# One Trainium2 core, a four-part transformer block: gate products placed between large products, some transposes issued by SyncE, earlier output weights

## The chip, the cores and the metric
The kernel runs on one core of a Trainium2 chip. The metric is device time in microseconds (us) of one execution, lower is better. A core has TensorE (PE; its weight loads are shown as PEld), VectorE (DVE), ScalarE (ACT), GpSimd (POOL) and SyncE (SP), each with a queue of its own, worked off in order; a queue can also issue DMAs (SPq, ACTq, POOLq).

## What is computed
Two batches of 512 tokens of 1024 features pass four sub-blocks, each added to the residual `x`:

```python
x = x + tanh(g_xattn[0]) * L0_xattn(layernorm(x), ctx)   # product of two fake-quantised matrices
x = x + tanh(g_ffn[0]) * L0_ffn(layernorm(x))            # W_org plus softmax-weighted LoRA experts
x = x + tanh(g_xattn[1]) * L1_xattn(layernorm(x), ctx)   # 32 query heads, 8 key heads, 1024 keys, then @ Wo
x = x + tanh(g_ffn[1]) * L1_ffn(layernorm(x))            # mixture of experts
# L1_ffn(h):
logits = concat([h, ratio]) @ gate_w + gate_b            # 3 experts; ratio = mean |h| of text / of vision rows
top_val, top_idx = top_k(softmax(logits), 2)             # the values are used per token,
expert(e) = act_e(h @ w1[e] + b1[e]) @ w2[e] + b2[e]     # the indices of token 0 for the whole batch
```

## The kernel before, in words
Every fp32 product is made of three bf16 ones (`triple`, L637): upper × upper, upper × lower, lower × upper part. The token rows stand in eight tiles of 128 (`TT` = 8, tiles 0 to 3 are batch 0). `XTh` and `XTl` hold the upper and lower parts of the normalised rows, transposed by DMA. A weight chunk of 128 rows is loaded by SyncE into one of the stages (`load_weights` L350, `load_expert` L477), gets its upper part from one engine and its lower part from GpSimd, and the semaphore `wt_done` counts finished chunks. All engines are programmed by hand, in program order, with semaphores between them.

The stages around the change, in order:

- **Queries.** 16 items (`query_item` L828) of 24 products of 512 columns, with score products of the first attention groups among them. An item goes to one of the four banks 6, 7, 2, 3; ScalarE copies the upper part (L1280), VectorE takes the lower (L1644, counted by `q_lo`), SyncE stores both to DRAM (`queries_out` L419). SyncE loads one chunk of the output weights `o` after every second item (L456); GpSimd splits it (L516, L518).
- **Attention groups.** 16 groups of 32 steps (`group` L933). A step has a score product (L866), whose maximum VectorE takes (L1616), and the transposed scores of another group (L948), exponentiated by ScalarE (L1261) into a ring of four buffers `PB`; every four steps `weigh` (L879) makes eight narrow fp32 products. GpSimd adds pairs of `PB` buffers (L607), four additions per group. The 17th exponential of a group sequence waits for the first addition, since it overwrites its input. Before group 0, TensorE waits for all 16 lower query halves (`q_lo`, L969).
- **Output tiles.** `output_tile(t)` (L915), 48 products each (L911), for tiles 0 to 7. VectorE updates `X` (L1664), takes mean and variance (`statistics`), ScalarE the root (`root` L1081), VectorE the reciprocal and `xn` (L1683). `rows_turned` (L1164) on ScalarE copies the upper part (L1173), issues its transpose (L1175), sums absolute values (L1178) and issues the transpose of the lower part (L1181), which VectorE makes (`lower_part`, L1595) once the lower transpose of the tile before has landed. In this order, the root of tile t+1 comes behind the lower transpose of tile t.
- **Gate.** `gate_logits(b)` (L975): for four tiles and eight feature chunks a `triple` with 3 output columns, 96 products, then one fp32 product with ones over the absolute sums (L986). `gate_logits(0)` stands between output tiles 5 and 6, `gate_logits(1)` behind the first four hidden tiles. VectorE's `choose_experts(b)` (L1709) needs both results and writes `idx`, which SyncE reads as the address of the expert's weights.
- **First layer of expert slot 0.** Four hidden tiles at once, chunk by chunk (k = 0 to 7, L1041), each k waiting for its w1 chunk; then hidden tiles 4 to 7 one by one (`hidden_tile` L1005), each waiting for the activation (ScalarE, L1319) four tiles before. For the first 16 expert chunks ScalarE makes the upper part (`weights_hi` L1291, L1295), GpSimd the lower (L629); chunks 0 to 11 stand in ScalarE's program among the rows of tiles 5 to 7 (L1304) and ahead of the activations. There are four stages, so the load of chunk c waits for `wt_done` of chunk c − 4. Chunks 8 to 15 are w2.
- Then the second layer, and the other three slots.

Of the kernel before, what the change touches and what calls it, by code (L numbers as in the profile page):

```python
# [14 lines left out]
BF16 = mybir.dt.bfloat16  # L15
# [5 lines left out]
P = 128  # L21
# [95 lines left out]
def build(nc, x, ctx_nat, ctx_t, wts, lora_q, lora_keys, scalars, gate_w, w1, b1, w2, b2, out):  # L117
    with ExitStack() as ctx:
        def sb(name, shape, dt):
            return ctx.enter_context(nc.sbuf_tensor(name, shape, dt))  # L120
# [41 lines left out]
        gwh = sb("gwh", [P, KT * EXPERTS], BF16)  # L162
        gwl = sb("gwl", [P, KT * EXPERTS], BF16)
# [470 lines left out]
        def _(pe):  # L634
# [298 lines left out]
            def group(g):  # L933

                for t in range(STEPS):
# [33 lines left out]
            pe.wait_ge(q_lo, B * KT)  # L969
# [5 lines left out]
            def gate_logits(b):  # L975
                rows_in_place(2, range(b * TB, (b + 1) * TB))
                pe.wait_ge(rt_read, b)
                for t in range(b * TB, (b + 1) * TB):
                    for k in range(KT):
                        cols = slice(k * D + t * P, k * D + (t + 1) * P)  # L980
                        e3 = slice(k * EXPERTS, (k + 1) * EXPERTS)
                        mm = triple([bank[6][:, t * EXPERTS:(t + 1) * EXPERTS]], XTh[:, cols], XTl[:, cols],
                                    [gwh[:, e3]], [gwl[:, e3]], k == 0, k == KT - 1)
                mm.then_inc(lg_mm, 1)
                pe.wait_ge(am_done, 4 * (b + 1))
                pe.matmul(bank[7][:, b * 2 * TB:(b + 1) * 2 * TB], onesf[:, :],  # L986
                          AM[:, b, :, :].rearrange("p a t -> p (a t)"), start=True, stop=True).then_inc(as_mm, 1)
# [53 lines left out]
            for k in range(KT):  # L1041
                pe.wait_ge(wt_done, W1_N(0) + k + 1)
                for f in range(4):
                    if k == 0 and f % 2 == 0:
                        pe.wait_ge(x_up, 6 * TT - 2 + f)
                    w = slice(k * D + f * P, k * D + (f + 1) * P)
                    mm = triple([bank[f][:, :]], w1_h[:, w], w1_l[:, w], [XTh[:, k * D:k * D + S]],
                                [XTl[:, k * D:k * D + S]], k == 0, k == KT - 1)
                    if k == KT - 1:
                        mm.then_inc(a_mm, 1)  # L1050
            gate_logits(1)
# [11 lines left out]
        def _(act):  # L1063
# [100 lines left out]
            def rows_turned(m, t, rooted=False, before_lower=lambda: None):  # L1164

                if not rooted:
                    root(TT + m, t % 2)
# [5 lines left out]
                act.activation(nat_h, xn[0][:, :], ACT.Copy).then_inc(nat_hi, 1)  # L1173
                act.wait_ge(nat_hi, m - TT + 1)
                act.dma_start_transpose(out=per_tile(XTh)[:, :, t * P:(t + 1) * P], in_=nat_h).then_inc(hi_t[t], 16)  # L1175
                if m >= 2 * TT:
                    act.wait_ge(abs_done, t + 1)
                    act.activation(junk, xn[0][:, :], ACT.Abs, accum_out=rowabs[:, t:t + 1]).then_inc(abs_done, 1)  # L1178
                before_lower()
                act.wait_ge(nat_lo, m - TT + 1)  # L1180
                act.dma_start_transpose(out=per_tile(XTl)[:, :, t * P:(t + 1) * P], in_=nat_l).then_inc(lo_t[t], 16)  # L1181

# [46 lines left out]
            for t in range(TT):  # L1229
                rows_turned(TT + t, t)  # L1230
# [66 lines left out]

            for t in range(TT - 3):
# [36 lines left out]
        def _(dve):  # L1335
# [103 lines left out]
            def gate_parts():  # L1439
                dve.wait_ge(const_in, 48)  # L1440
                dve.tensor_copy(gwh[:, :], gwf[:, :]).then_inc(qc_step, 1)
                dve.wait_ge(qc_step, 10)
                dve.tensor_tensor(gwl[:, :], gwf[:, :], gwh[:, :], ALU.subtract).then_inc(qc_step, 1)
# [214 lines left out]
            def output_norm(t):  # L1658
# [7 lines left out]
                dve.wait_ge(x_up, 2 * (m + 1))  # L1666
                statistics(m + TT, x_tile(t), t % 2)
# [41 lines left out]
            def choose_experts(b):  # L1709
# [12 lines left out]
                nxt(dve.tensor_tensor(L[:, tiles, :],  # L1722
                                      bank[6][:, b * TB * EXPERTS:(b + 1) * TB * EXPERTS].rearrange("p (t e) -> p t e", e=EXPERTS),
                                      rb[:, b:b + 1, :].to_broadcast([P, TB, EXPERTS]), ALU.add))
# [151 lines left out]
```

## Time and profile before
| | |
|---|---|
| three runs | 1251.49, 1257.41, 1254.35 us; median 1254.35 |
| the profiled execution | 1259.31 us, its span 1257.5 us, mean granted TensorE clock 0.993 |
| busy: TensorE, VectorE, GpSimd, ScalarE | 1222.9, 821.9, 681.7, 476.4 us |

The span runs from the first to the last instruction. Matmul records of 512 columns show about 0.38 us each, but successive ones start 0.216 us apart; distances between starts are what counts. The granted clock is 1.0 at 2.4 GHz and 0.5 at 1.2 GHz.

### The profile page before, as it was taken

What the parts mean: (1) busy time and instruction counts of PE and PEld (TensorE: products, weight loads), DVE (VectorE), ACT (ScalarE), POOL (GpSimd) and SP (SyncE); (2) the same over time, 40 slices, a digit from 0 to 9 for tenths busy, and PEclk for the clock granted to TensorE, in tenths of its full rate; (3) what the DMA queues carried; (4) which work ended last, traced back from release to release, by engine and by line L of the source; (5) the groups of instructions that cost most, each with busy time, mean ns of one, the idle gap of its engine ahead of it and who ended that gap; (6) DMA issues with size and microseconds to landing.
All of it is one profiled execution on the core that took longest, in us unless ns stands there. A gap on an engine that the chain in (4) does not pass through costs nothing.

```text
span 1257.5 us, 16924 instructions
## 1 busy us (share of the span) xinstructions
PE 1222.9 (97%) x6504; PEld 512.1 (41%) x6504; DVE 821.9 (65%) x1417; ACT 476.4 (38%) x826; POOL 681.7 (54%) x300
## 2 busy tenths in 40 slices
PE   8998899999999899999999999999989999999998
PEld 6564444444444322222222222234434444444444
DVE  7997731433456778998999989335538855737622
ACT  4774521000100467777777677743242010010000
POOL 6005898500033478888989889870164553624510
PEclk9999999999999999999999999999989999999999
DMA  9566143311332145453545444443493443523301
GB/s 356 171 245 154 65 134 115 86 34 34 79 129 92 59 96 113 107 117 87 120 106 112 95 103 104 84 84 60 113 213 105 140 126 100 184 85 101 117 15 52
DMA packets 86764, 141.20 MB, mean 112 GB/s; under 512 B 49056, under 2 KB 59296, under 8 KB 82592
## 3 DMA queue, kind: packets, MB, share of 16 engines
q1 hardware_dynamic: 45840, 94.03, 23.7%
q0 software_dynamic: 4608, 33.56, 13.2%
q10 hardware_dynamic: 36240, 12.60, 5.2%
q8 instruction: 48, 0.79, 0.3%
q14 instruction: 28, 0.23, 0.1%
HBM read 85.49 MB, written 10.49 MB: 76 GB/s over the span
## 4 chain that ended last, share of the span: by engine, by line
PE 79%; DVE 12%; DMA 2%; POOL 2%; ACT 2%; issue 1%; ACTq 0%; SPq 0%; POOLq 0%; DVEq 0%
PE bank L641 46%; PE bank L879 9%; DVE mxp L1616 8%; PE bank L866 6%; PE bank L948 5%; PE bank L911 5%; PE bank L666 3%; PE bank L672 3%; DVE xn L1606 2%; DMA stage_c<-w_in 1%; DMA R<-R 1%; POOL R L607 1%; POOL R L629 1%; PE bank L720 1%; POOL X L548 1%
## 5 line engine op out<-in xcount | busy, mean ns | idle before, releaser
L1616 DVE TENSOR_REDUCE mxp<-bank 128x1 f32<-128x512 f32 x512 | 320.6, 680 | 60.6 <-PE bank L866 60.3
L1261 ACT ACTIVATE R<-bank 128x512 f32<-128x512 f32 x512 | 273.9, 602 | 116.7 <-PE bank L948 113.5
L641 PE MATMUL bank<-XTh,R 128*128 128x512 bf16 x896 | 279.3, 381 | 4.7 <-POOL R L629 4.5
L607 POOL TENSOR_TENSOR R<-R 128x2048 f32<-128x2048 f32 x48 | 218.6, 4555 | 35.4 <-ACT R L1261 29.4
L641 PE MATMUL bank<-R 128*128 128x512 bf16 x960 | 209.2, 379 | 0.0
L641 PE MATMUL bank<-XTl,R 128*128 128x512 bf16 x448 | 170.7, 381 | 0.0
L629 POOL TENSOR_TENSOR R<-stage_pair,R 128x1024 bf16<-128x1024 f32 x32 | 75.4, 2371 | 138.6 <-DVE R L1770 84.1
L641 PEld LDWEIGHTS bank<-R 128*128 128x128 bf16 x960 | 93.9, 98 | 113.3
L866 PE MATMUL bank<-R 96*128 96x512 bf16 x352 | 134.6, 382 | 4.6 <-DVE mxp L1616 3.0
L879 PE MATMUL bank<-R,stage_c 128*32 128x512 f32 x1024 | 137.1, 607 | 0.5 <-ACT R L1261 0.5
L948 PE MATMUL bank<-R 98*128 98x512 bf16 x352 | 134.4, 382 | 2.1 <-ACT R L1261 2.1
L641 PEld LDWEIGHTS bank<-XTh,R 128*128 128x128 bf16 x896 | 88.0, 98 | 112.1 <-POOL R L629 5.4
L516 POOL TENSOR_TENSOR R<-stage_pair,zero 128x1024 f32 (+1 forms) x35 | 67.2, 1920 | 77.4 <-DMA stage_pair<-wts_in 74.5
L629 POOL TENSOR_TENSOR R<-stage_c,R 128x1024 bf16<-128x1024 f32 x32 | 73.7, 2315 | 59.8 <-DVE R L1770 50.2
L1319 ACT ACTIVATE R<-bank,b1t 128x512 f32<-128x512 f32 x32 | 21.6, 686 | 198.1 <-PE bank L641 198.1
L866 PEld LDWEIGHTS bank<-R 96*128 96x128 bf16 x352 | 34.2, 97 | 112.2 <-DVE mxp L1616 84.7
L518 POOL TENSOR_TENSOR R<-stage_pair,R 128x1024 f32 (+1 forms) x35 | 75.9, 2167 | 5.3 <-POOL R L516 4.7
L1606 DVE RECIPROCAL xn<-p_total 128x128 f32<-128x128 f32 x64 | 59.2, 937 | 27.6 <-POOL xn L589 27.6
L607 POOL TENSOR_TENSOR stage_pair<-R 128x2048 f32<-128x2048 f32 x16 | 73.7, 4604 | 4.3 <-ACT R L1261 3.2
L911 PE MATMUL bank<-R,XTh 128*128 128x512 bf16 x256 | 69.7, 379 | 0.8 <-issue 0.8
L1815 DVE SCALAR_TENSOR_TENSOR X<-xn,TV,X 128x512 f32<-128x512 f32 x32 | 67.4, 2147 | 0.1
L1084 ACT ACTIVATE lnv<-lnv 128x1 f32<-128x1 f32 x32 | 6.5, 202 | 158.7 <-DVE lnv L1365 138.3
(194 smaller groups left out, 1502.0 us busy)
## 6 DMA issues: line engine op xcount, KB each, us to landing
stage_pair<-wts_in SPq DMA_DIRECT2D x35, 512.0 KB, 3.7
R<-R POOLq DMA_DIRECT2D x16, 1024.0 KB, 6.9
stage_pair<-R POOLq DMA_DIRECT2D x16, 1024.0 KB, 7.0
stage_pair<-w_in SPq DMA_DIRECT2D x32, 512.0 KB, 3.5
stage_c<-w_in SPq DMA_DIRECT2D x32, 512.0 KB, 3.6
R<-q_scr SPq DMA_DIRECT2D x48, 128.0 KB, 2.4
XTh<-ctx_t_in SPq DMA_DIRECT2D x11, 512.0 KB, 7.7
XTh<-ctx_nat_in SPq DMA_DIRECT2D x9, 512.0 KB, 3.9
```

Source lines behind the costliest of these rows:

```text
L518: pool.tensor_tensor(lo, stage_w[stage][:, :], hi, ALU.subtract).then_inc(wt_done, 1)
L607: pool.tensor_tensor(PS[(0, 1, 2, 1)[j]], PB[2 * j % 4], PB[2 * j % 4 + 1], ALU.add).then_inc(p_add, 1)
L629: pool.tensor_tensor(lo[:, cols], stage_e[(n - N_WT) % RING_E][:, :], hi[:, cols], ALU.subtract).then_inc(wt_done, 1)
L641: mm = pe.matmul(o, a, m, start=first and a is ah and bs is bh, stop=last and a is al)
L866: pe.matmul(bank[s_bank(u)][:, :], QS[g % 3][0:96, h * S + qt * P:h * S + (qt + 1) * P], KS[g % 3][0:96, kh * HALF:(kh + 1) * HALF], start ...
L879: mm = pe.matmul(out_bank[h * HD:(h + 1) * HD, :], weights, probs[:, h * S:(h + 1) * S], start=first, stop=last)
L911: mm = pe.matmul(outs[h], a[i][:, cols], b[i][:, k * D + h * HALF:k * D + (h + 1) * HALF], start=k == 0 and i == 0, stop=k == KT - 1 and i ...
L948: pe.matmul(bank[t_bank(g, t)][:, :], KS[g % 3][0:98, kt * P:(kt + 1) * P], QS[g % 3][0:98, h * S:(h + 1) * S], start=True, stop=True).the ...
L1261: act.activation(PB[kt % 4][:, h * S:(h + 1) * S], bank[t_bank(g, t)][:, :], ACT.Exp, scale=float(HD) ** -0.5).then_inc(exp_done, 1)
L1606: dve.reciprocal(rec[:, cols], p_sum[:, cols]).then_inc(rec_done, 1)
L1616: dve.tensor_reduce(mxp[head // REP % 2][:, m, n // 2, n % 2:n % 2 + 1], bank[s_bank(u)][:, :], AX.X, ALU.max).then_inc(s_max, 1)
L1815: dve.scalar_tensor_tensor(out=xh, in0=b2b[:, hc], scalar=TV[:, j * TT + t:j * TT + t + 1], in1=xh, op0=ALU.mult, op1=ALU.add).then_inc(eo ...
```

## The change
1. Gate products: upper and lower gate weights stand side by side in one tile `gwb`, so that per tile and chunk there are two products (`XTh` with 6 columns, `XTl` with 3) instead of three. They are issued one at a time, each behind a large product: for batch 0 behind the 48 of output tile 5 and the first 16 of tile 6, for batch 1 among the hidden tiles' `triple`s and, the last 16, behind them. VectorE adds the two column sets in one more small operation. Chunks 6 and 7 of the first layer are taken tile by tile, with one wait for both.
2. SyncE issues both transposes of tiles 5, 6 and 7, among the loads of w1 chunks 4 to 7 and ahead of those of w2; it waits for the transposes of tile 4 first. ScalarE only makes the upper parts, and has another order of conversions.
3. ScalarE takes the root of tile t+1 ahead of the lower transpose of tile t; VectorE updates `X` for tile 5 ahead of the expert choice.
4. The `o` weights are loaded after each of the first eight query items. Group 0 starts at 14 lower query halves; its first two steps wait for 15 and 16.

```diff
@@ SyncE
-                if c % 2 == 1:
-                    load_weights(WT_AT["o"] + item // 2, 1)
+                if item < KT:
+                    load_weights(WT_AT["o"] + item, 1)
...
+            def turn_upper(t):
+                sp.wait_ge(nat_hi, TT + t + 1)
+                sp.dma_start_transpose(out=per_tile(XTh)[:, :, t * P:(t + 1) * P], in_=nat_h).then_inc(hi_t[t], 16)
+
+            def turn_lower(t):
+                sp.wait_ge(nat_lo, TT + t + 1)
+                sp.dma_start_transpose(out=per_tile(XTl)[:, :, t * P:(t + 1) * P], in_=nat_l).then_inc(lo_t[t], 16)
+
             e = expert(0)
-            load_expert(W1_N(0), w1, e, 0, KT)
+            load_expert(W1_N(0), w1, e, 0, RING_E)
+            sp.wait_ge(hi_t[TT - 4], 32)
+            sp.wait_ge(lo_t[TT - 4], 32)
+            turn_upper(TT - 3)
+            turn_lower(TT - 3)
+            load_expert(W1_N(0), w1, e, RING_E, RING_E + 1)
+            turn_upper(TT - 2)
+            load_expert(W1_N(0), w1, e, RING_E + 1, KT)
+            turn_lower(TT - 2)
+            turn_upper(TT - 1)
+            turn_lower(TT - 1)
@@ TensorE
-            def output_tile(t):
+            def output_tile(t, gate_parts=range(0)):
...
                 for k in range(KT):
-                    mm = output_part(t, k, 0, 6)
-                mm.then_inc(nat_mm, 1)
+                    for n in range(6):
+                        mm = output_part(t, k, n, n + 1)
+                        if k == KT - 1 and n == 5:
+                            mm.then_inc(nat_mm, 1)
+                        if 6 * k + n < len(gate_parts):
+                            gate_part(0, gate_parts[6 * k + n])
...
+                    elif STEPS * g + t < 2:
+                        pe.wait_ge(q_lo, B * KT - 1 + t)
...
-            pe.wait_ge(q_lo, B * KT)
+            pe.wait_ge(q_lo, B * KT - 2)
...
-            def gate_logits(b):
...
+            def gate_part(b, n):
+
+                t, k, low = b * TB + n // (2 * KT), n // 2 % KT, n % 2
+                if n % (2 * KT) == 0:
+                    rows_in_place(2, range(t, t + 1))
+                if n == 0:
+                    pe.wait_ge(rt_read, b)
+                cols = slice(k * D + t * P, k * D + (t + 1) * P)
+                count = EXPERTS if low else 2 * EXPERTS
+                mm = pe.matmul(bank[6][:, 2 * t * EXPERTS:2 * t * EXPERTS + count], (XTl if low else XTh)[:, cols],
+                               gwb[:, 2 * k * EXPERTS:2 * k * EXPERTS + count], start=k == 0 and not low,
+                               stop=k == KT - 1 and low == 1, skip_group_check=True)
+                if n == 2 * KT * TB - 1:
+                    mm.then_inc(lg_mm, 1)
...
-            for t in range(TB, TT - 2):
-                output_tile(t)
-            gate_logits(0)
-            for t in range(TT - 2, TT):
-                output_tile(t)
+            output_tile(TB)
+            output_tile(TB + 1, range(0, 48))
+            output_tile(TB + 2, range(48, 64))
+            output_tile(TB + 3)
...
+            for k in range(KT - 2):
                 pe.wait_ge(wt_done, W1_N(0) + k + 1)
                 for f in range(4):
...
-            gate_logits(1)
+                    first_part(f, k)
+                    if k < 4:
+                        gate_part(1, 8 * k + 2 * f)
+                        gate_part(1, 8 * k + 2 * f + 1)
+            pe.wait_ge(wt_done, W1_N(0) + KT)
+            for f in range(4):
+                for k in range(KT - 2, KT):
+                    first_part(f, k)
+                    gate_part(1, 32 + 4 * f + 2 * (k - KT + 2))
+                    gate_part(1, 33 + 4 * f + 2 * (k - KT + 2))
+            for n in range(48, 64):
+                gate_part(1, n)
@@ ScalarE
             for t in range(TT - 3):
-                if t == 0:
-                    divided_hi(GROUPS - 1)
-                rows_turned(2 * TT + t, t, rooted=t == 0)
+                if t > 0:
+                    root(3 * TT + t, t % 2)
+                    turn_lower(2 * TT + t - 1, t - 1)
+                rows_upper(2 * TT + t, t)
+                turn_upper(2 * TT + t, t)
+                absolute_sum(t)
+            root(4 * TT - 3, 1)
+            turn_lower(3 * TT - 4, TT - 4)
...
-            for t, before, after in ((TT - 3, (0, 2), (2, 2)), (TT - 2, (4, 2), (6, 1)), (TT - 1, (7, 1), (8, 4))):
-                rows_turned(2 * TT + t, t, before_lower=lambda before=before: weights_hi(*before))
-                weights_hi(*after)
+            rows_upper(3 * TT - 3, TT - 3)
+            absolute_sum(TT - 3)
+            root(4 * TT - 2, 0)
+            weights_hi(0, 2)
+            rows_upper(3 * TT - 2, TT - 2)
+            absolute_sum(TT - 2)
+            weights_hi(2, 2)
+            root(4 * TT - 1, 1)
+            weights_hi(4, 2)
+            rows_upper(3 * TT - 1, TT - 1)
+            absolute_sum(TT - 1)
+            weights_hi(6, 6)
@@ VectorE
             for t in range(TB + 1):
+                output_up(t)
                 output_norm(t)
             absolute_sums(0)
+            output_up(TB + 1)
             choose_experts(0)
-            for t in range(TB + 1, TT):
+            output_norm(TB + 1)
+            for t in range(TB + 2, TT):
+                output_up(t)
                 output_norm(t)
```

## Rows read from the trace of the kernel before

**Rows 1.** the page: the span of the profiled execution
```profile
span 1257.5 us, 16924 instructions
```
**Rows 2.** the chain of waits in order of time: start us, us, what
```profile
425.58 3.75 DMA stage_pair<-wts_in
...
914.52 10.35 DMA stage_c<-w_in
...
933.29 2.13 POOL R L629
...
943.42 310.83 PE bank L641 x1440
```
**Rows 3.** TensorE in time, 424 to 443: start, us, what, [idle before <- releaser]
```profile
424.77 0.39 PE L866 MATMUL bank<-R 96*128 96x512 bf16 x1 [1.42 <-DVE R L1644]
...
433.97 1.06 PE L879 MATMUL bank<-R,stage_c 128*32 128x512 f32 x8
...
438.93 0.39 PE L948 MATMUL bank<-R 98*128 98x512 bf16 x1 [2.06 <-ACT R L1261]
439.25 1.80 PE L879 MATMUL bank<-R,stage_c 128*32 128x512 f32 x8
...
442.98 0.38 PE L948 MATMUL bank<-R 98*128 98x512 bf16 x1
```
**Rows 4.** GpSimd in order of time, 429 to 443 us
```profile
429.50 1.89 POOL L516 TENSOR_TENSOR R<-stage_pair,zero 128x1024 f32 x1 [8.05 <-DMA stage_pair<-wts_in]
...
433.65 8.99 POOL L607 TENSOR_TENSOR R<-R 128x2048 f32<-128x2048 f32 x2
```
**Rows 5.** ScalarE in order of time, 429 to 439 us
```profile
429.92 2.06 ACT L1261 ACTIVATE R<-bank 128x512 f32<-128x512 f32 x4 [0.94 <-PE bank L948]
...
438.28 0.60 ACT L1261 ACTIVATE R<-bank 128x512 f32<-128x512 f32 x1 [2.07 <-POOL R L607]
```
**Rows 6.** TensorE in time, the first gate group, 888 to 891 us
```profile
888.86 0.17 PE L641 MATMUL bank<-gwh,XTh 128*128 128x3 bf16 x1
...
891.28 0.37 PE L986 MATMUL bank<-AM,onesf 128*128 128x8 f32 x2
```
**Rows 7.** TensorE in order of time, the stop at the eighth first-layer weight
```profile
935.46 0.61 PE L641 MATMUL bank<-XTh,R 128*128 128x512 bf16 x1 [4.50 <-POOL R L629]
...
940.56 0.21 PE L641 MATMUL bank<-gwh,XTh 128*128 128x3 bf16 x1
```
**Rows 8.** DMA issues of 918 to 919.4 us: us from issue to landing
```profile
XTl<-xn ACTq DMA_TRANSPOSE x1, 13.3
```
**Rows 9.** all engines in order of time, first product behind the second gate group
```profile
943.16 0.18 PEld L641 LDWEIGHTS bank<-XTh,R 128*128 128x128 bf16 x1
943.27 0.38 PE L641 MATMUL bank<-XTh,R 128*128 128x512 bf16 x1
```
**Rows 10.** VectorE in order of time, 895 to 912 us
```profile
895.15 0.16 DVE L1738 CAST idx<-idxf 1x2 int32<-1x2 f32 x1
...
898.30 1.22 DVE L1595 TENSOR_TENSOR xn<-xn 128x1024 bf16<-128x1024 f32 x1
...
911.56 0.81 DVE L1683 TENSOR_SCALAR xn<-X,mv,lnv 128x1024 f32<-128x1024 f32 x1
```
**Rows 11.** SyncE's queue in order of time: first load of an expert's weights
```profile
896.11 0.95 SPq L481 DMA_DIRECT2D stage_pair<-w_in  x2
```
**Rows 12.** DMA issues, 898 to 902 us: KB, us from issue to landing
```profile
stage_c<-w_in SPq DMA_DIRECT2D x1, 512.0 KB, 6.9
XTl<-xn ACTq DMA_TRANSPOSE x1, 6.2
```
**Rows 13.** ScalarE and its queue in order of time, 915 to 941 us
```profile
915.85 1.04 ACT L1295 ACTIVATE R<-stage_pair 128x1024 bf16<-128x1024 f32 x1
...
918.37 1.25 ACTq L1181 DMA_TRANSPOSE XTl<-xn  x1
...
940.25 1.28 ACT L1319 ACT_TABLE_LOAD   x1
```

More of the change, by code:

```diff
@@ L161, in build @@
         gwf = sb("gwf", [P, KT * EXPERTS], F32)
-        gwh = sb("gwh", [P, KT * EXPERTS], BF16)
-        gwl = sb("gwl", [P, KT * EXPERTS], BF16)
+        gwb = sb("gwb", [P, KT * 2 * EXPERTS], BF16)
         b1t = sb("b1t", [P, EXPERTS * KT], F32)
@@ L972, in _ @@
                 group(g)
-            def gate_logits(b):
[L976 to L987, printed above, removed]
+            def gate_part(b, n):
[11 more added lines that the diff above has]
+                    mm.then_inc(lg_mm, 1)
+                    pe.wait_ge(am_done, 4 * (b + 1))
+                    pe.matmul(bank[7][:, b * 2 * TB:(b + 1) * 2 * TB], onesf[:, :],
+                              AM[:, b, :, :].rearrange("p a t -> p (a t)"), start=True, stop=True).then_inc(as_mm, 1)
             weigh(GROUPS - 1, KT - 1)
@@ L1038, in second_layer, with first_part @@
                         mm.then_inc(b_half if halves == (0,) else b_mm, 1)
-            for k in range(KT):
+            def first_part(f, k):
+                if k == 0 and f % 2 == 0:
+                    pe.wait_ge(x_up, 6 * TT - 2 + f)
+                w = slice(k * D + f * P, k * D + (f + 1) * P)
+                mm = triple([bank[f][:, :]], w1_h[:, w], w1_l[:, w], [XTh[:, k * D:k * D + S]],
+                            [XTl[:, k * D:k * D + S]], k == 0, k == KT - 1)
+                if k == KT - 1:
+                    mm.then_inc(a_mm, 1)
+            for k in range(KT - 2):
                 pe.wait_ge(wt_done, W1_N(0) + k + 1)
                 for f in range(4):
[L1044 to L1050, printed above, removed]
-            gate_logits(1)
+                    first_part(f, k)
[10 more added lines that the diff above has]
+                gate_part(1, n)
             for f in range(4, KT):
@@ L1162, in _, with rows_upper @@
             act.wait_ge(const_in, 48)
-            def rows_turned(m, t, rooted=False, before_lower=lambda: None):
-                if not rooted:
-                    root(TT + m, t % 2)
+            def rows_upper(m, t):
                 act.wait_ge(xn_done, TT + m + 1)
@@ L1173, in rows_turned, with turn_upper, turn_lower, absolute_sum @@
                 act.activation(nat_h, xn[0][:, :], ACT.Copy).then_inc(nat_hi, 1)
+            def turn_upper(m, t):
                 act.wait_ge(nat_hi, m - TT + 1)
                 act.dma_start_transpose(out=per_tile(XTh)[:, :, t * P:(t + 1) * P], in_=nat_h).then_inc(hi_t[t], 16)
[L1176 to L1179, printed above, removed]
+            def turn_lower(m, t):
                 act.wait_ge(nat_lo, m - TT + 1)
                 act.dma_start_transpose(out=per_tile(XTl)[:, :, t * P:(t + 1) * P], in_=nat_l).then_inc(lo_t[t], 16)
+            def absolute_sum(t):
+                act.wait_ge(abs_done, t + 1)
+                act.activation(junk, xn[0][:, :], ACT.Abs, accum_out=rowabs[:, t:t + 1]).then_inc(abs_done, 1)
             def scale_rows(t):
@@ L1229, in _ @@
             for t in range(TT):
-                rows_turned(TT + t, t)
+                root(2 * TT + t, t % 2)
+                rows_upper(TT + t, t)
+                turn_upper(TT + t, t)
+                turn_lower(TT + t, t)
             def row_out(g):
@@ L1296, in weights_hi @@
                                    ACT.Copy).then_inc(ew_act, 1)
+            divided_hi(GROUPS - 1)
             for t in range(TT - 3):
[L1299 to L1301 removed]
+                if t > 0:
[6 more added lines that the diff above has]
+            turn_lower(3 * TT - 4, TT - 4)
             act.wait_ge(pv_mm, KT * GROUPS)
             act.wait_ge(p_add, KT // 2 * GROUPS)
[L1304 to L1306 removed]
+            rows_upper(3 * TT - 3, TT - 3)
[10 more added lines that the diff above has]
+            weights_hi(6, 6)
             reg = act.alloc_register("expert_act")
@@ L1440, in gate_parts @@
                 dve.wait_ge(const_in, 48)
-                dve.tensor_copy(gwh[:, :], gwf[:, :]).then_inc(qc_step, 1)
+                full = gwf[:, :].rearrange("p (k e) -> p k e", k=KT)
+                gw_h, gw_l = (gwb[:, :].rearrange("p (k i e) -> p i k e", k=KT, i=2)[:, i, :, :] for i in range(2))
+                dve.tensor_copy(gw_h, full).then_inc(qc_step, 1)
                 dve.wait_ge(qc_step, 10)
-                dve.tensor_tensor(gwl[:, :], gwf[:, :], gwh[:, :], ALU.subtract).then_inc(qc_step, 1)
+                dve.tensor_tensor(gw_l, full, gw_h, ALU.subtract).then_inc(qc_step, 1)
             def x_step(t):
@@ L1656, in _, with output_up @@
                 invert(GROUPS - 2, quarter)
-            def output_norm(t):
+            def output_up(t):
                 m = 2 * TT + t
@@ L1666, in output_norm @@
                 dve.wait_ge(x_up, 2 * (m + 1))
+            def output_norm(t):
+                m = 2 * TT + t
                 statistics(m + TT, x_tile(t), t % 2)
@@ L1721, in choose_experts @@
                 dve.wait_ge(lg_mm, b + 1)
-                nxt(dve.tensor_tensor(L[:, tiles, :],
-                                      bank[6][:, b * TB * EXPERTS:(b + 1) * TB * EXPERTS].rearrange("p (t e) -> p t e", e=EXPERTS),
-                                      rb[:, b:b + 1, :].to_broadcast([P, TB, EXPERTS]), ALU.add))
+                logits = bank[6][:, 2 * b * TB * EXPERTS:2 * (b + 1) * TB * EXPERTS].rearrange("p (t i e) -> p i t e", i=2, e=EXPERTS)
+                nxt(dve.tensor_tensor(L[:, tiles, :], logits[:, 0, :, :], rb[:, b:b + 1, :].to_broadcast([P, TB, EXPERTS]), ALU.add))
+                nxt(dve.tensor_tensor(L[:, tiles, :], logits[:, 1, :, :], L[:, tiles, :], ALU.add))
                 f0, f1, f2 = (L[0:1, b * TB, e:e + 1] for e in range(EXPERTS))
```

## The prediction

> **What bounds the kernel now.** The page gives one core, a span of 1257.5 us [rows 1] and TensorE busy almost all of it, so I read the chain of waits first and asked where it leaves TensorE. It leaves it for other engines in two places that the change touches: through the DMA and GpSimd work of the `o` weights at 425 us, and through the first expert's weights at 914 to 935 us. From 943.42 us to the end it is TensorE alone, 1440 products of 512 columns in 310.83 us, 0.216 us each [rows 2]. Hence whatever moves the 943.42 moves the end by as much.
>
> Stop A. Where the queries end, TensorE idles 1.42 us for the last lower query half. At 438.93 it idles again, 2.06 us, and then runs slowly: eight attention products take 1.80 us where 1.06 is usual [rows 3]. The releaser is ScalarE, which had itself waited 2.07 us for GpSimd: the 17th exponential overwrites a buffer that GpSimd's first pair addition reads. GpSimd starts that addition at 433.65 because the last of the `o` weights came late (it had idled 8.05 us for the DMA) and was split until then [rows 4]. The eighth exponential had ended at about 430.5 [rows 5].
>
> Gate burst. The first group of gate products runs from 888.86 to 891.28, 96 products in 2.42 us, 25 ns each; with its ones product TensorE is away from large products for 2.6 us [rows 6]. The second costs as much.
>
> Stop B. The eighth chunk of w1 holds TensorE idle for 4.50 us. Then twelve large products take 5.10 us (935.46 to 940.56) where 12 × 0.216 = 2.6 is usual: after the idle time the granted clock is the lower level, 1.2 GHz, and 2.5 us go there [rows 7]. The views show why the chunk is late. ScalarE converts it only behind the row work of the last tile, GpSimd subtracts after that (ending at 933.29 + 2.13 = 935.4), and loads issued from SyncE while ScalarE issued transposes crawled: one load 10.35 us [rows 2], one transpose 13.3 us [rows 8].
>
> **The change, part by part.**
>
> (a) `o` weights, one per query item for the first eight items. SyncE's queue then waits at most for GpSimd's 4 us split, less than a query item of 24 products (5.2 us), so the query stores behind it are not held. The last split ends some 45 us earlier. GpSimd's first addition starts at 430.5 instead of 433.65, takes 8.99 / 2 = 4.5 us and ends at 435.0. The 17th exponential could run at about 436.2 (438.28 − 2.07). That leaves 1.2 us of cover; if it goes, the stop returns by what is missing. Gain: 2.06 idle, plus the slow stretch. From 438.93 to 442.98 stand one large product (0.3 with the load behind it), eight attention products (1.0 to the next start) and five large ones (1.08), 2.4 us at full clock against 4.05 taken, so 1.65. Together **−3.7**. What is late next is nothing that I can find: GpSimd has 4.5 us of work per 5.7 us of TensorE's.
>
> (b) Group 0 no longer waits for all queries. TensorE could start 1.42 us earlier, but ScalarE's exponentials can't: they stand behind the last query copy and a table load. I take **−0.15**; ends 0 and −1.4.
>
> (c) Gate products. Per half 64 instead of 96, as both weight halves stand side by side (6 columns), so 128 in all. What one costs between large products no row shows. Lower bound 0, if its 3 or 6 columns vanish in the pipeline. Upper bound 0.11: behind the ones product, the load for the next large product starts at 943.16 and the product at 943.27 [rows 9]. I take 25 ns, because in the burst too every product had a fresh 128-column load behind the one before it, the same pair of steps. 128 × 0.025 = 3.2 against 2 × 2.42: −1.6.
> That a load costs its whole length is also what the Trainium skill states ("TensorE: Matmul & The Clock Gate", section LDWEIGHTS (loading the stationary operand)): time is columns over 1.2 per ns, 107 ns for 128 columns. By that rule this part would cost 13.7 and save 4.8, so +8.9; the burst at 25 ns speaks against it, the row at 0.11 us for it.
>
> (d) Transposes, roots, order of ScalarE. TensorE's needs: tile 5 with 48 gate parts ends at 890.1 (888.86 + 1.2), the last 16 gate parts with tile 6's first 16 products at 893.9, tile 7 ends at 911.4, chunk 8 is needed at 911.4 + 0.3 + 72 × 0.216 + 32 × 0.025 = 928.1. The supply: experts are chosen from the gate sums, 3.9 us after the ones product of 891.28 (`idx` cast at 895.15 [rows 10], plus one small addition), now 898.2. SyncE's first load was 0.8 us behind [rows 11], now 899.0: 2.9 us later than before. Between `idx` and the lower part of tile 4 stood an update and the statistics (895.31 to 898.30 [rows 10]); the update is now ahead of the choice, about 1.6 us are left, so the lower transpose of tile 4 goes out at 898.2 + 1.6 + 1.2 = 901.1, among these loads, and took 6.2 us there (the fourth load 6.9) [rows 12]: landed about 908. Now VectorE's lower part of tile 5 (1.22), its root steps and scaling (about 1 + 0.81 [rows 10]), and ScalarE's copy and absolute sum (1.04 to 1.25 each) follow, until 913.5. Chunks 2 and 3 are converted, 1.04 each [rows 13], until 915.5. GpSimd, 2.13 per chunk, ends chunk 3 at 918.8; chunk 7 is loaded at 918.9, lands within 3.7 and is ready after four more subtractions, 918.8 + 4 × 2.1 = 927.2. Needed at 928.1: stop B goes, with 0.9 us of cover. TensorE would then reach the fifth hidden tile at 928.1 + 24 × 0.216 + 32 × 0.025 + 0.3 = 934.4 instead of 943.42 (5.2 more for products, 0.8 for gate parts).
>
> What is late next is the second layer's first loads, 8 to 11. They are now behind both last transposes in SyncE's queue, and ScalarE must convert them before its first activation, for which the fifth hidden tile waits. The lower transpose of tile 6 goes out at 919.3 behind chunk 7 and lands at 924; VectorE's last lower part ends at 925.2; the last transpose (1.25 to issue [rows 13]) leaves at 926.5; four loads are issued until 928.3 and land by about 934 (6.9 for four [rows 12], less some for an empty queue); then 1.04 to convert, 1.28 for the table [rows 13], 0.6 for the activation: **937.7**, give or take 1.5. TensorE idles 934.4 to 937.7. After 2.06 and 4.50 idle it came back at 1.2 GHz and lost 1.65 and 2.5, after 1.42 it didn't; for 3.3 I take 1.7. Part (d) with (c): 937.7 + 1.7 − 943.4 = **−4.0**.
>
> Roots ahead of lower turns save about 1.3 us per tile on VectorE, which no product waits for until tile 7; the supply above already has them. The extra small addition in the expert choice is in it too.
>
> **Sum**, against the profiled execution of 1259.3: −3.7 − 0.15 − 4.0 = −7.9, 1251.4. The median shown, 1254.35, is 5 us below that execution; with the same difference it becomes **1246.5**.
>
> **The rivals.**
> 1. No new wait. If loads 8 to 11 land 3 us sooner (they have the queue to themselves), 934.4 stands: −9.0 − 3.85 = −12.9, 1241.5. For it: one load alone landed in 3.75 us [rows 2]. Against: six steps in a row must all be short.
> 2. Loads shown. Each gate part costs 0.11: the fifth hidden tile is reached at 934.4 + 128 × 0.085 = 945.3, later than the supply, which the later gate sums (64 × 0.085 = 5.4) put at 943.1. +1.9 − 3.85 = −2.0: 1252.4. The Trainium skill's rule cited under (c) would have it so.
> 3. SyncE's single queue. A transpose among loads takes 13.3 us [rows 8] instead of 6.2; all that follows is 7 us later, the stop at chunk 8 stays at about 6 us, the fifth hidden tile comes at 944.8 and the slow clock adds 2.5: +3.9 − 3.85 = 0: 1254.4.
> 4. Slower. A gate part between large products drains the pipeline: its own 0.17 us [rows 6] and then the load of the next, 0.1. Then 0.26 each, 934.4 + 128 × 0.235 = 964.5: +21.1 − 3.85 = +17: 1271.6. It decides from 0.125 us per part on, and by over 0.5% from 0.175. Against it: the burst overlapped these.
> 5. The change does not do what it says in (a): exponentials still meet a busy GpSimd. Then only −4.2: 1250.2.
>
> **How the numbers follow.** Forecast 0.45, rival 1 0.25, rival 2 0.10, rival 3 0.10, rival 4 0.05, rival 5 0.05. The kernel's three runs span 6 us, so about 0.5% (6.3 us) is what a measurement can tell. The forecast's own range is −5 to −11 (1.5 us either way in the supply, with or without the slow clock): four fifths of it lie beyond 6.3. Faster 0.36 + 0.25 = 0.61, same 0.09 + 0.25 = 0.34, slower 0.05. The range takes rival 1 with 1.5 us for the runs' spread, 1240, and reaches to rival 2, 1252.5.
>
> **What would show it.** (a) No idle time of TensorE behind a GpSimd addition near 437, and the `o` splits done by 390. (c) The distance between large products with a gate part between: 0.24 if right, 0.33 or more for rival 2, 0.45 for rival 4. (d) No wait for chunk 8; a wait of the fifth hidden tile for an activation that follows a conversion of load 11, and the 1.2 GHz level after it. It is wrong if that wait is missing, if the stop at chunk 8 remains, or if gate parts cost above 0.1.

## The result and the profile after

After the change the kernel takes 1253.94 us (median of 20 runs, 1252.47 to 1256.13), beside 1256.83 us for the kernel before on the same chip (20 runs, 1251.49 to 1263.28). The ratio is 0.9978, 95% interval 0.9969 to 0.9986: a gain of 2.9 us, where 7.9 was forecast. The profiled execution took 1253.30 us.

The page of the kernel after: span, and busy time, share and instructions of each engine:

```profile
span 1251.5 us, 16801 instructions
...
PE 1217.8 (97%) x6440; PEld 510.3 (41%) x6440; DVE 828.0 (66%) x1419; ACT 476.0 (38%) x826; POOL 683.8 (55%) x300
```

The profiled pair differs by 6.0 us in span [rows 1], the medians by 2.9: the profiled execution of before is 2.5 us above its median of 20 runs and that of after 0.6 below its own. So the pair is cut into stretches first. Each is measured between the same two products on both sides:

| stretch | before | after | difference | forecast |
|---|---|---|---|---|
| start to the last query product | 422.98 | 420.87 | −2.1 | 0 |
| from there to the start of output tile 1 | 411.3 | 406.7 | −4.6 | −3.85, (a) and (b) |
| from there to the fifth hidden tile | 109.2 | 106.85 | −2.3 | −5.7 |
| from there to the end | 310.83 | 313.82 | +3.0 | +1.7 |

Of the change the first stretch holds only the earlier `o` loads, and experiment 1, which has them too, is 0.2 us from before at its end (422.77). Of its 2.1 us, 1.8 arise at 53 us, where TensorE waits about as long in both kernels and is slow behind it in one and not in the other (granted clock 0.60 from 53.5 to 57.8 us before, 1.00 from 53.4 to 56.1 after). TensorE in order of time, the kernel before:

```profile
53.54 4.44 PE L666 MATMUL bank<-R 128*128 128x512 bf16 x12 [2.10 <-DVE R L1409]
```

The same view of the kernel after:

```profile
53.42 2.75 PE L684 MATMUL bank<-R 128*128 128x512 bf16 x12 [2.56 <-DVE R L1470]
```

Stop A [rows 3, 4, 5] is gone. GpSimd now starts its first pair addition as soon as the eighth exponential is done, and the only wait of TensorE that the profile lists around there is 0.76 us, where 1.42 stood ahead of group 0. GpSimd in order of time, the first addition:

```profile
428.04 4.54 POOL L625 TENSOR_TENSOR R<-R 128x2048 f32<-128x2048 f32 x1 [45.95 <-ACT R L1307]
```

TensorE in order of time, its one wait from 418 to 445 us:

```profile
422.66 0.39 PE L972 MATMUL bank<-R 98*128 98x512 bf16 x1 [0.76 <-DVE R L1707]
```

TensorE in output tile 5, a large product (L929), a gate product (L1008) and the next large one:

```profile
872.09 0.38 PE L929 MATMUL bank<-R,XTh 128*128 128x512 bf16 x1
872.30 0.17 PE L1008 MATMUL bank<-gwb,XTl 128*128 128x3 bf16 x1
872.33 0.38 PE L929 MATMUL bank<-R,XTh 128*128 128x512 bf16 x1
```

A gate product between two large ones adds 0.024 us: the two start 0.24 us apart (872.09, 872.33) instead of 0.216.

Stop B [rows 7] has become four waits. Up to the stretch in question the after trace runs 6.67 us ahead of the before trace (output tile 1 starts at 827.58 and at 834.25), so add 6.67 to compare with the times of the prediction. TensorE in order of time:

```profile
907.48 0.39 PE L659 MATMUL bank<-XTh,R 128*128 128x512 bf16 x1 [1.19 <-DVE X L1727]
...
912.37 0.39 PE L659 MATMUL bank<-XTh,R 128*128 128x512 bf16 x1 [0.56 <-POOL R L647]
...
924.23 0.39 PE L659 MATMUL bank<-XTh,R 128*128 128x512 bf16 x1 [0.92 <-POOL R L647]
...
934.43 0.61 PE L659 MATMUL bank<-XTh,R 128*128 128x512 bf16 x1 [3.83 <-ACT R L1380]
```

The last wait is the largest, 3.83 us for ScalarE's first activation (L1380), and it is as the prediction had it: the activation stands behind the conversions (L1341) of chunks 8 to 11, and these behind their loads. ScalarE in order of time:

```profile
927.35 1.06 ACT L1341 ACTIVATE R<-stage_pair 128x1024 bf16<-128x1024 f32 x1 [7.23 <-DMA stage_pair<-w_in]
...
931.32 1.06 ACT L1341 ACTIVATE R<-stage_c 128x1024 bf16<-128x1024 f32 x1 [0.21 <-DMA stage_c<-w_in]
...
933.68 1.84 ACT L1380 ACTIVATE R<-bank,b1t 128x512 f32<-128x512 f32 x3
```

Busy times in the stretch behind the wait (a time and a count for each engine; PEclk is the granted clock):

```profile
core 0: us, PE busy (x) PEld busy (x) DVE busy (x) ACT busy (x) POOL busy (x), PEclk, DMA share, GB/s
...
934.40:940.30 5.90, 5.87 (x15) 2.10 (x16) 5.66 (x9) 3.65 (x6) 5.63 (x4) 0.51 0.78 248
```

For 5.9 us the granted clock is 0.51, so TensorE is at 1.2 GHz.

The chain of waits of after, behind the gate sums, shows what sets the time of the activation: the lower transpose of tile 4, VectorE, ScalarE, GpSimd's six subtractions, then the loads of w2.

```profile
894.38 7.07 DMA XTl<-xn
901.55 2.02 DVE xn L1658
904.42 1.69 DVE xn L1750
...
909.26 14.93 POOL R L647 x6
925.14 6.16 DMA stage_c<-w_in
932.39 1.28 ACT L1380
934.43 313.82 PE bank L659 x1440
```

### The profile page after: what moved, and what is told of

Its sections match the earlier page's. It is cut to its first block, busy times and chain, and to the rows that moved or that the text cites. A ratio compares the mean times of both kernels' runs of the same rounds, so it can differ in the third digit from the quotient of the medians.

```text
span 1251.5 us, 16801 instructions
## 1 busy us (share of the span) xinstructions
PE 1217.8 (97%) x6440; PEld 510.3 (41%) x6440; DVE 828.0 (66%) x1419; ACT 476.0 (38%) x826; POOL 683.8 (55%) x300
## 3 DMA queue, kind: packets, MB, share of 16 engines
q0 software_dynamic: 4608, 33.56, 13.3%
## 4 chain that ended last, share of the span: by engine, by line
PE 77%; DVE 16%; ACT 2%; issue 2%; DMA 2%; POOL 1%; SPq 0%; DVEq 0%; ACTq 0%; POOLq 0%
PE bank L659 46%; PE bank L897 10%; DVE mxp L1679 8%; PE bank L884 7%; PE bank L972 6%; PE bank L929 5%; DVE xn L1669 2%; PE bank L690 2%; PE bank L684 2%; POOL R L647 1%; DVE R L1406 1%; DVE stats L1419 1%; DMA XTl<-xn 1%; DMA stage_c<-ctx_t_in 1%; DMA stage_c<-w_in 0%
## 5 line engine op out<-in xcount | busy, mean ns | idle before, releaser
L1380 ACT ACTIVATE R<-bank,b1t 128x512 f32<-128x512 f32 x32 | 21.7, 687 | 198.9 <-PE bank L659 198.8
L884 PEld LDWEIGHTS bank<-R 96*128 96x128 bf16 x352 | 34.1, 97 | 109.2 <-DVE mxp L1679 84.2
L929 PE MATMUL bank<-R,XTh 128*128 128x512 bf16 x256 | 70.5, 379 | 0.8 <-issue 0.8
L1867 DVE CAST R<-R 128x512 bf16<-128x512 f32 x32 | 17.5, 548 | 75.7 <-ACT R L1380 75.7
```

The costliest lines, as they stand in the source:

```text
L884: pe.matmul(bank[s_bank(u)][:, :], QS[g % 3][0:96, h * S + qt * P:h * S + (qt + 1) * P], KS[g % 3][0:96, kh * HALF:(kh + 1) * HALF], start ...
L929: mm = pe.matmul(outs[h], a[i][:, cols], b[i][:, k * D + h * HALF:k * D + (h + 1) * HALF], start=k == 0 and i == 0, stop=k == KT - 1 and i ...
```

## The experiments

Theory A: (a) gives what it was to give, and (d) with (c) gives nothing as it stands, because the weights come late and then the w2 conversions ahead of the first activation open a stop that costs its 3.8 us and 3 us of slow clock. Theory B: the missing 5 us are the price of the gate products. The letters are those of the prediction. Each experiment is a copy of before, of after or of experiment 3, with the edit named. All were timed beside the kernel before.

### 1. The `o` weights alone

```diff
-                if c % 2 == 1:
-                    load_weights(WT_AT["o"] + item // 2, 1)
+                if item < KT:
+                    load_weights(WT_AT["o"] + item, 1)
```


> The kernel before with part (a) alone: one chunk of the o weights after each of the first eight query items. Theory A (the sum of the prediction holds for this part): the stop at the 17th exponential (2.06 us) and the slow stretch behind it (1.65 us) go, the time falls by 3.7 us, ratio 0.997. Rival: the stop is an accident of one execution, or its time comes back later in the groups; then less than 1 us. In the trace GpSimd's first addition starts within 1 us of the eighth exponential's end.

1253.55 us (12 runs), ratio 0.9970, 0.9959 to 0.9982: −3.3 us against 1256.85. GpSimd's additions show the cause as in after:

```profile
430.48 4.53 POOL L607 TENSOR_TENSOR R<-R 128x2048 f32<-128x2048 f32 x1 [46.30 <-ACT R L1261]
```

Between traces, the distance from the last query product to the second product that turns the score maxima (`identf`) is 463.57 − 422.98 = 40.6 us before, 459.54 − 422.77 = 36.8 here, 457.11 − 420.87 = 36.2 after. So (a) is worth 3.8 and (b) 0.5. The kernel with (a) alone is as fast as the whole change, as far as the intervals tell (0.9959 to 0.9982 beside 0.9969 to 0.9986).

### 2. The gate products alone

Only part 1 of the change, on before.

> The kernel before with the gate products of the changed kernel alone (two instead of three per tile and chunk, spread), everything else as before. Theory A: 0.025 us each, so TensorE does 1.6 us less for itself; but the expert choice comes about 3 us later, and with it the weights of the first layer, whose eighth chunk TensorE waits for. So the stop at that chunk grows by 1 to 4 us and the time stays or gets longer by up to 3 us. Rival: the gate products were the cost; then 1.6 us less, ratio 0.9987.

1258.38 us (11 runs), ratio 1.0009, 0.9999 to 1.0019. By themselves the spread products gain nothing, though they should save 1.6 us of TensorE. My reading is that the later choice of the experts takes it back; experiments 5 and 7 bear on that. The trace of this kernel doesn't show it: its execution, 1254.85 us, is the fastest of the 11. The stop at the eighth chunk has not grown there, as I had expected, but shrunk from 4.50 to 0.52 us, with waits of 0.97 (chunk), 2.50 (update of `X`) and 0.32 us (activation) beside it, and the granted clock from 935 to 950 us is 1.00. Where the median loses its time stands in no trace.

### 3. w2 conversions behind the activations

On after: ScalarE converts chunks 8 to 11 behind the four activations instead of ahead of them.

```diff
-            weights_hi(6, 6)
+            weights_hi(6, 2)
...
-                                weights_hi(12, 4)
+                                weights_hi(8, 8)
```


> The changed kernel, but ScalarE converts chunks 8 to 11 behind the first four activations instead of ahead of them. Theory A (the loss of the changed kernel is that the fifth hidden tile waits for an activation which stands behind those conversions): the idle time of 3.8 us and the 3.0 us of the 1.2 GHz stretch go, 6.8 us less than the changed kernel, about 1247.1 us against its 1253.9. Rival: the stop only moves, because activations 4 to 7 and with them the second layer then come late; no gain, or under 2 us.

1247.34 us (6 runs), ratio 0.9925, 0.9912 to 0.9938. This is 6.6 us below after, the 3.8 of the wait and the 3.0 behind it. ScalarE in order of time, the last of the four activations (L1380) and the first w2 conversions (L1341):

```profile
931.48 0.69 ACT L1380 ACTIVATE R<-bank,b1t 128x512 f32<-128x512 f32 x1 [0.71 <-PE bank L659]
932.07 1.99 ACT L1341 ACTIVATE R<-stage_pair 128x1024 bf16<-128x1024 f32 x2
```

All that TensorE waited for from 880 to 960 us (total, times, longest); no activation is among it:

```profile
PE bank L659 <- POOL R L647: 1.5, 2, 0.9
PE bank L659 <- DVE X L1727: 1.2, 1, 1.2
```

### 4. The same stop, filled

On after: 17 products of 512 columns, which nothing reads, stand where TensorE idles.

```diff
+            for n in range(17):
+                pe.matmul(bank[4][:, :], w1_h[:, 0:P], XTh[:, 0:S], start=True, stop=True)
             for f in range(4, KT):
                 hidden_tile(0, 0, f)
```


> The changed kernel with 17 products of 512 columns, whose result nothing reads, between the last gate product and the fifth hidden tile: they fill 3.7 of its 3.8 us of idle time. Theory A (idle time brings the clock to 1.2 GHz, and that costs 3.0 us behind it): the fifth hidden tile starts when it did, at full clock, and the time falls by 3.0 us against the changed kernel. Rival: the lower clock is not due to that idle time; then no change.

1250.84 us (6 runs), ratio 0.9959, 0.9946 to 0.9973: 3.1 us below after on the medians (2.4 by the ratios), though the fifth hidden tile starts no sooner (934.71). TensorE, the filler (16 of its 17 records are in the trace) and what follows at 0.216 us per product:

```profile
930.91 3.83 PE L1094 MATMUL bank<-XTh,R 128*128 128x512 bf16 x16
934.71 0.39 PE L659 MATMUL bank<-XTh,R 128*128 128x512 bf16 x1
934.94 0.38 PE L659 MATMUL bank<-XTl,R 128*128 128x512 bf16 x1
```

So the stop has two prices: 3.8 us of idle time, which experiment 3 takes back with the rest, and about 3 us of slow clock, which goes when TensorE stays busy. Between traces, from the fifth hidden tile to the end of the span, it is 314.2 us here and 317.1 in after, 2.9 less.

### 5. The change without its part (d)

On after, with the transposes, roots, ScalarE's and VectorE's order as before.

> The changed kernel with part (d) undone: ScalarE issues all transposes, its and VectorE's order are those of before; o weights, the start of group 0 and the spread gate products stay. Theory A (parts add up): before, less 3.3 us (e1_o_early), plus 1.2 us (e2_gates_only), 1254.8 us; so part (d), as it stands in the changed kernel, is worth 1 us and no more, because what it saves at the eighth chunk it loses at the fifth hidden tile. Rival: without (d) the changed kernel would be slower than before, over 1257 us, and (d) is what pays.

1255.00 us (12 runs), ratio 0.9986, 0.9970 to 1.0002. The medians give (d), as it stands, about 1 us, and the intervals (after has 0.9969 to 0.9986) don't tell that from nothing. Without it the stop for a w1 chunk is back at its old size:

```profile
930.58 0.61 PE L641 MATMUL bank<-XTh,R 128*128 128x512 bf16 x1 [4.85 <-POOL R L629]
```

Two more waits stand ahead of it, 0.98 us for a chunk and 2.50 us for the update of `X`, so TensorE waits 8.3 us in the first layer, where before waits 4.7. The weights and updates come late for a TensorE that has gained time, which fits the reading of experiment 2. (d) shortens these waits and opens the one for the activation.

### 6. The transpose of tile 4 ahead of half the loads

On experiment 3: SyncE loads two chunks, waits for tile 4's transposes, issues the upper one of tile 5, and loads the other two.

```diff
-            load_expert(W1_N(0), w1, e, 0, RING_E)
+            load_expert(W1_N(0), w1, e, 0, 2)
             sp.wait_ge(hi_t[TT - 4], 32)
             sp.wait_ge(lo_t[TT - 4], 32)
             turn_upper(TT - 3)
+            load_expert(W1_N(0), w1, e, 2, RING_E)
```


> e3_w2_behind_acts, with SyncE loading only chunks 0 and 1 before it waits for the transposes of tile 4, and chunks 2 and 3 behind the upper transpose of tile 5. Theory A (the lower transpose of tile 4 lands late, 7.1 us, because four loads are ahead of it, and VectorE's wait for it causes TensorE's waits of 1.2, 0.6 and 0.9 us in the first layer): it lands within 5 us, the 1.2 us wait goes, time 1.2 to 2.7 us less than e3, 1244.6 to 1246.1. Rival: chunks 2 and 3 come late instead; same time or up to 2 us longer.

1245.15 us (6 runs), ratio 0.9905, 0.9886 to 0.9925. TensorE waits for nothing in the first layer. The lower transpose of tile 4 took 7.1 us from issue to landing in after and 4.1 here (last number of these DMA issues of 893 to 896 us). After:

```profile
XTl<-xn ACTq DMA_TRANSPOSE x1, 7.1
```

This kernel:

```profile
XTl<-xn ACTq DMA_TRANSPOSE x1, 4.1
```

### 7. The gate products in one block again

On experiment 3: the 64 gate products of batch 0, still in the form of the change, stand together behind output tile 5.

```diff
-            output_tile(TB + 1, range(0, 48))
-            output_tile(TB + 2, range(48, 64))
+            output_tile(TB + 1)
+            for n in range(64):
+                gate_part(0, n)
+            output_tile(TB + 2)
```


> e3_w2_behind_acts, with the 64 gate products of batch 0 together behind output tile 5 instead of spread over tiles 5 and 6. Theory A (a gate product costs 0.025 us wherever it stands, and only its lateness matters): the expert choice comes 3.4 us earlier, the first layer's waits of 2.7 us in all go, time 2 to 2.7 us less than e3, about 1245. Rival (spreading hides part of the gate products' cost): the same time as e3 or up to 1.6 us more.

1245.67 us (6 runs), ratio 0.9905, 0.9886 to 0.9924: 1.7 us below experiment 3. One wait of 0.3 us is left in the first layer, of 2.7 in all; the expert's index is written at 890.08 us instead of 892.90. So the spreading costs here what it delays the choice of the experts.

### 8. Both

On experiment 3, with the edits of 6 and 7.

> e7_gates_together with the load order of e6_two_loads_first. Theory A: e7 already leaves no wait in the first layer, so within 0.5 us of e7. Rival: each has a wait of its own, and both together are faster than either by 1 us or more.

1245.14 us (6 runs), ratio 0.9905, 0.9885 to 0.9924. The two repairs don't add up, since either takes away the same waits. Experiments 6 to 8 are the fastest of all: 1% below before and 0.7% below after. Their intervals overlap that of experiment 3 (0.9912 to 0.9938), so the 1.7 to 2.2 us between them rest on the medians and on the waits that are gone from the traces.

### 9. GpSimd held back once

The rows of after show VectorE's and GpSimd's work longer where they meet (the next section has them). On experiment 3, GpSimd's first subtraction waits for VectorE's scaling of tile 6:

```diff
+                if n == N_WT:
+                    pool.wait_ge(xn_done, 3 * TT + 7)
                 if n < W1_N(1):
                     pool.wait_ge(ew_act, n - N_WT + 1)
```


> The kernel with w2 conversions behind the activations, with one more wait: GpSimd's subtraction for chunk 0 waits until VectorE has scaled the rows of tile 6. There, without the wait, VectorE's lower part of tile 5 took 1.94 us and the scaling 1.68, while GpSimd's two subtractions took 5.19. Theory A, one engine holds the other off: their excess is the other's work. With the wait nothing runs beside them, so lower part 1.22, scaling 0.81, 1.5 us sooner done in all, and TensorE's wait of 1.2 us for the update of X goes. GpSimd's first subtraction then takes 2.1; it starts some 4 us later, and the two may still meet VectorE's lower part of tile 6. Theory B, something else slows both in this stretch (transfers among them): the lower part stays near 1.9 and the scaling near 1.7, and the wait of 1.2 us stays. The time itself says little: chunk 7 still comes when GpSimd has done chunks 2 to 7, whose start moves by at most 0.5 us either way, so 1246 to 1249 by both theories.

1247.10 us (4 runs), ratio 0.9929, 0.9910 to 0.9948: no other time than experiment 3, but other rows. VectorE in order of time in experiment 3:

```profile
903.11 1.94 DVE L1658 TENSOR_TENSOR xn<-xn 128x1024 bf16<-128x1024 f32 x1 [2.53 <-DMA XTl<-xn]
905.91 1.68 DVE L1750 TENSOR_SCALAR xn<-X,mv,lnv 128x1024 f32<-128x1024 f32 x1
```

GpSimd in experiment 3:

```profile
901.85 5.19 POOL L647 TENSOR_TENSOR R<-stage_pair,R 128x1024 bf16<-128x1024 f32 x2 [52.55 <-ACT R L1341]
```

VectorE in this kernel:

```profile
903.50 1.23 DVE L1660 TENSOR_TENSOR xn<-xn 128x1024 bf16<-128x1024 f32 x1 [2.19 <-DMA XTl<-xn]
905.58 0.81 DVE L1752 TENSOR_SCALAR xn<-X,mv,lnv 128x1024 f32<-128x1024 f32 x1
```

GpSimd in this kernel:

```profile
906.47 4.23 POOL L649 TENSOR_TENSOR R<-stage_pair,R 128x1024 bf16<-128x1024 f32 x2 [56.47 <-DVE xn L1752]
```

1.94 became 1.23, 1.68 became 0.81, 5.19 became 4.23. The transfers around them were much the same (four loads by SyncE until 896.5, the same two transposes from 903.5 on), so theory A of this run holds for this meeting: the two engines hold each other off. One expectation failed. TensorE's wait for the update of `X` went, but a wait of 1.54 us for the now later chunk 0 took its place, and the sum of its waits was 2.1 us (2.7 in experiment 3), where I had not asked what chunk 0's delay would cost.

## Why the prediction was wrong

The time, 1253.94 us, was outside the range of 1240 to 1252.5. The steps, one by one:

**(a), forecast −3.7: right.** Experiment 1 measured −3.3 on the medians and −3.8 between traces, by the mechanism named. Rival 5 falls.

**(b), forecast −0.15: too small.** It is −0.5. TensorE's wait fell from 1.42 [rows 3] to 0.76 us. ScalarE's exponentials start only 0.12 us sooner behind the last query product (2.32 instead of 2.44 us), as forecast. But its idle time behind the first seven fell from 0.94 [rows 5] to 0.55 us, which the forecast had left out.

**(c), 0.025 us per gate product: right.** The rows at 872 us give 0.024. Rivals 2 and 4 fall, which needed 0.11 and 0.26. The weight load of 0.11 us in [rows 9] is hidden between large products. The load time that the prediction took from the Trainium skill is thus no price to be added, and its section gives a load's time without saying that it adds to the products'. The same page ("TensorE: Matmul & The Clock Gate") says in its section "Step-by-step: what each phase is for" that the next weights load while the running product streams, and in "Back-to-back issue gap" that a product of up to 64 columns takes about 25 ns; the rows agree with both.

**(d) with (c), forecast −4.0: this is the step that failed.** It gave +0.7 in the profiled pair (−2.3 and +3.0). The prediction got the new stop, its place and its releaser right, and mis-sized two terms of its sum, by 3.4 and 1.3 us:

1. *The fifth hidden tile came 3.4 us later than forecast*, at 934.43 + 6.67 = 941.1 instead of 937.7. The transpose of tile 4 still landed as forecast (901.45 + 6.67 = 908.1; forecast about 908), so rival 3 falls. From there on the supply was reckoned with durations that an engine has when it is alone. Three rows of VectorE show it. Two stand in the chain above, at 901.55 and 904.42; the third, in VectorE's order of time:

```profile
920.17 2.02 DVE L1658 TENSOR_TENSOR xn<-xn 128x1024 bf16<-128x1024 f32 x1 [7.31 <-DMA XTl<-xn]
```

GpSimd in order of time, two subtractions to a row:

```profile
900.36 5.20 POOL L647 TENSOR_TENSOR R<-stage_pair,R 128x1024 bf16<-128x1024 f32 x2 [52.42 <-ACT R L1341]
909.26 5.60 POOL L647 TENSOR_TENSOR R<-stage_c,R 128x1024 bf16<-128x1024 f32 x2 [3.70 <-ACT R L1341]
...
918.98 5.19 POOL L647 TENSOR_TENSOR R<-stage_c,R 128x1024 bf16<-128x1024 f32 x2
```

The lower part of tile 5 took 2.02 us instead of 1.22 and the scaling of tile 6 1.69 instead of 0.81 [rows 10]: 1.7 us. GpSimd's chunks 2 and 3 took 5.60 instead of 4.2, 1.4 us more; its 914.86 releases the load of chunk 7 in SyncE's queue, and the lower transpose of tile 6 stands behind it. The last lower part took 2.02 again, 0.8 us. Together 3.9 us, by rows, and the loads of chunks 8 to 11 went out at 923.56 + 6.67 = 930.2 instead of 926.5, 3.7 us late. SyncE's queue in order of time:

```profile
912.48 2.87 SPq L480 DMA_DIRECT2D stage_c<-w_in  x2
915.40 1.24 SPq L493 DMA_TRANSPOSE XTl<-xn  x1
...
922.22 1.23 SPq L493 DMA_TRANSPOSE XTl<-xn  x1
923.56 1.01 SPq L480 DMA_DIRECT2D stage_pair<-w_in  x2
```

From there to the fifth hidden tile it was 10.9 us, forecast 11.2. The chain above comes to the w2 loads by GpSimd instead, and it is as late: chunk 7 is done at 924.17 + 6.67 = 930.8, forecast 927.2. At the first meeting each excess is the rest of the other engine's instruction: GpSimd's first subtraction, 4.21 / 2 = 2.1 us long when alone, would end at 902.46; VectorE's 1.22 us behind it ends at 903.68, measured 903.57; GpSimd's second then ends at 905.7, measured 905.56. The scaling doesn't come out as well: 905.56 + 0.81 = 906.4, measured 906.1. Experiment 9 shows that the excess goes when they do not meet. The Trainium skill ("SBUF — State Buffer", section Who interferes with whom) states that a VectorE instruction with two SBUF inputs contends with a GpSimd one that reads SBUF, and calls contention for the ports they share an exclusive lock; the rows of the lower parts agree. The forecast set VectorE's lower part of tile 5 at 908 and did not ask what GpSimd did then: its first two subtractions, from 900.36 + 6.67 = 907.0 on. The trace of before already held such a meeting, 3.6 us behind the end of [rows 10], from which the forecast took its 1.22 and 0.81 us. VectorE in order of time, before:

```profile
915.52 2.02 DVE L1595 TENSOR_TENSOR xn<-xn 128x1024 bf16<-128x1024 f32 x1
```

GpSimd in order of time, before:

```profile
911.69 4.75 POOL L629 TENSOR_TENSOR R<-stage_c,R 128x1024 bf16<-128x1024 f32 x2
```

That the meetings made the first activation of after late is read from these rows and sums; no run has after without them. In experiment 9, where one meeting is gone and no conversion stands ahead of the activation, the time stayed the same.

2. *The slow clock cost 3.0 us instead of 1.7.* TensorE idled 3.83 us. Experiment 4 measures the price by itself, 3.1 us on the medians and 2.9 between traces. The 1.7 was chosen for an idle time of 3.3 us, near the 1.65 that followed 2.06 us and not the 2.5 that followed 4.50; no run had shown it.

On top, TensorE itself was 2.7 us later than forecast at the end of the gate products, 1.19 + 0.56 + 0.92 of waits; the larger wait for the activation covers that. Rival 1 (no new wait) falls for the change as made. Experiment 6 reaches what it described, a fifth hidden tile without a wait, by another order of ScalarE and SyncE, and came out 11.6 us below before, where rival 1 had 12.9.

**Profile and median.** In the profiled pair (a) to (d) give −4.6 + 0.7 = −3.9; the medians give −2.9. The slow stretch behind 53 us, up to 2 us, stands in four of the eleven traces (before and experiments 1, 7 and 9) and makes the last microsecond of either number uncertain. What the prediction did with its own execution (difference onto the median) was sound, but its median was that of three runs, 1254.35; 20 runs gave 1256.83. So of the 7.4 us between 1246.5 and 1253.94, 5.0 are the sum's and 2.5 that median's. Onto 1256.83 the same sum gives 1248.9, and the range would have reached to 1255.0, past the measured time; the sum would have been as wrong.

**Open:** whether both edits in (d), roots and transposes, gain; neither was run by itself. Also how much of the 3.4 us after would get back if VectorE and GpSimd did not meet. And why the clock falls behind the wait at 53 us in some executions alone.

## What to carry to other kernels

When a timetable of several engines is written, lay VectorE's and GpSimd's instructions over one another and charge each meeting with the rest of the other's instruction: by the rows, such meetings made the supply 3.7 us late here, where the forecast gain was 4.0. Look at what stands in a helper's queue ahead of the first result that TensorE needs: conversions that only the second layer needed, four hidden tiles later, stood ahead of an activation, and moving them back gave 6.6 us, more than the whole change. And a part that moves small work into the shadow of large work is paid with its result coming later, so ask who waits for that result.

## What was not expected of the hardware

- The fall of the granted clock behind an idle time is not the same each time. At 53 us a wait of 2.10 us was followed by 12 products in 4.44 us, and one of 2.56 us by 12 in 2.75; in other variants 2.31 and 2.65 us passed without a fall, 2.17, 2.46 and 2.75 us with one.
- Behind 3.83 us of idle time the low clock cost 2.9 to 3.1 us, behind 4.50 us it had cost 2.5 [rows 7].
- VectorE's scaling, with one large input, was also lengthened by GpSimd, 0.81 to 1.68 us, and back to 0.81 where they did not meet (experiment 9).
- Transposes in the queue of the loads landed sooner: the six issued by SyncE in after took 3.0 to 4.7 us, where ScalarE's among SyncE's loads took 13.3 [rows 8] and 6.2 [rows 12] before, 7.1 in after and 4.1 in experiment 6. What was in flight beside them differs, and no run changes the queue alone, so that the queue is the reason isn't shown. DMA issues of 914 to 925 us in after:

```profile
XTl<-xn SPq DMA_TRANSPOSE x2, 3.9
XTh<-xn SPq DMA_TRANSPOSE x1, 4.2
```
